# Three elementwise instructions of a weight quantiser, moved from VectorE to GpSimd beside attention

## The reference, cut to what matters

```python
def _weight_quant(w):                       # w_gate, w_up: 4096 x 1024, w_down: 1024 x 4096
    scale = 1.0 / clip(mean(abs(w)), 1e-05)
    wq = clip(round(w * scale), -1.0, 1.0) / scale
    return w + stop_gradient(wq - w)
def _act_quant(x):
    scale = 127.0 / clip(max(abs(x), axis=-1), 1e-05)
    return clip(round(x * scale), -128.0, 127.0) / scale     # the value of it
def _bitlinear(x, w): return einsum('bsi,oi->bso', _act_quant(x), _weight_quant(w))

xn = layernorm(x)
attn = softmax(q k^T / 16) v @ Wo.T         # 8 heads of 256; k, v from a latent of 64
ffn  = _bitlinear(silu(_bitlinear(xn, w_gate)) * _bitlinear(xn, w_up), w_down)
out  = x + attn + ffn
```

## Time and profile before

| | us |
|---|---|
| median of 2 runs | 5789.53 (5685.05 and 5894.02) |
| profiled execution | 5426.39 |
| its span, slowest core | 5424.8 |
| spans of the 8 cores | 5410.8 to 5424.8 |
| PE busy in the span | 4204.7 |
| DVE busy | 2171.8 |
| ACT busy | 2088.7 |
| POOL busy | 602.9 |

### The profile page before, as it was taken

How to read it: one execution, slowest core, us unless ns; L and a number is a source line. 1 busy time by engine, 2 the same in 40 slices (tenths; PEclk the granted TensorE clock), 3 DMA queues, 4 the chain that set the end, 5 groups by cost and what they waited for, 6 DMA issues and landing times.

```text
span 5424.8 us, 91608 instructions; the slowest of 8 cores (5410.8 to 5424.8 us)
## 1 busy us (share of the span) xinstructions
PE 4204.7 (78%) x24244; PEld 2326.7 (43%) x24244; DVE 2171.8 (40%) x2977; ACT 2088.7 (39%) x3427; POOL 602.9 (11%) x517
## 2 busy tenths in 40 slices
PE   1123399797997989979899795688888888099999
PEld 1121156364563645636456363343444433044444
DVE  5545511313113131131321311599999999111111
ACT  4324466263562635626356263233333333000000
POOL 1000000000000000000000000233333333000000
PEclk8556599898998989979899898898998989599999
DMA  4664311011110111101111212111111111355454
GB/s 126 156 159 125 130 35 44 26 44 36 34 44 26 44 36 34 44 26 44 36 34 44 80 52 63 47 36 40 32 38 40 30 40 28 76 160 134 123 130 109
DMA packets 535678, 350.52 MB, mean 65 GB/s; under 512 B 441920, under 2 KB 486976, under 8 KB 535168
## 3 DMA queue, kind: packets, MB, share of 16 engines
q1 hardware_dynamic: 464736, 155.77, 12.1%
q0 software_dynamic: 31824, 92.95, 6.7%
q10 hardware_dynamic: 38608, 95.96, 5.3%
HBM read 244.61 MB, written 109.05 MB: 65 GB/s over the span
## 4 chain that ended last, share of the span: by engine, by line
PE 60%; DVE 20%; DMA 7%; issue 7%; ACT 4%; SPq 1%; DVEq 1%; ACTq 0%; POOLq 0%; POOL 0%
PE psF L763 17%; PE psF L752 16%; PE psF L1061 8%; PE psF L395 4%; PE psF L939 4%; PE psF L945 3%; DMA arC<-x 3%; PE psF L1047 3%; DVE rsc L480 3%; DVE rsc L477 3%; DVE arB L483 2%; DVE t L471 2%; ACT arB L778 2%; DVE arB L445 2%; DVE smf L963 2%
## 5 line engine op out<-in xcount | busy, mean ns | idle before, releaser
L757 ACT ACTIVATE arB<-psF 128x512 bf16<-128x512 f32 x2048 | 1216.0, 597 | 1283.5 <-PE psF L752 1062.5
L763 PE MATMUL psF<-arB 128*128 128x257 bf16 x8192 | 1280.7, 278 | 97.1 <-ACT arB L778 95.0
L752 PE MATMUL psF<-arB 128*128 128x512 bf16 x4096 | 1237.8, 390 | 18.3 <-DVE arB L445 18.3
L763 PEld LDWEIGHTS psF<-arB 128*128 128x128 bf16 x8192 | 782.3, 99 | 537.6 <-issue 178.6
L945 PE MATMUL psF<-arB 128*128 128x512 bf16 x2048 | 493.4, 385 | 75.1 <-DMA arB<-wuT_d 75.1
L939 PE MATMUL psF<-arA,arB 128*128 128x512 bf16 x2048 | 536.1, 409 | 6.4 <-DMA arB<-xnqT_d 6.4
L959 POOL TENSOR_TENSOR arC<-arC 128x512 f32<-128x512 f32 x256 | 425.7, 1663 | 831.5 <-ACT arC L956 831.5
L1061 PE MATMUL psF<-arB,arA 128*128 128x512 bf16 x2048 | 451.0, 381 | 71.1 <-DMA arB<-wdT_d 70.9
L772 DVE RECIPROCAL smf<-psF 128x1 f32<-128x1 f32 x256 | 43.1, 168 | 1123.0 <-PE psF L763 1103.3
L752 PEld LDWEIGHTS psF<-arB 128*128 128x128 bf16 x4096 | 408.3, 100 | 108.9 <-issue 28.4
L951 ACT ACTIVATE arC<-psF,smf 128x512 f32<-128x512 f32 x256 | 175.9, 687 | 714.6 <-PE psF L945 614.5
(11 more groups left out here) (125 smaller groups left out, 3533.4 us busy)
## 6 DMA issues: line engine op xcount, KB each, us to landing
hqT_d<-p1b SPq DMA_DIRECT2D x32, 1024.0 KB, 6.2
arA<-hqT_d SPq DMA_DIRECT2D x32, 1024.0 KB, 7.0
arC<-Wg ACTq DMA_DIRECT2D x32, 512.0 KB, 5.9
arC<-x SPq DMA_DIRECT2D x32, 512.0 KB, 7.3
arC<-Wu ACTq DMA_DIRECT2D x32, 512.0 KB, 6.9
arC<-Wd ACTq DMA_DIRECT2D x32, 512.0 KB, 4.8
arC<-Wg POOLq DMA_DIRECT2D x32, 512.0 KB, 5.3
aoT_d<-arB SPq DMA_DIRECT2D x64, 256.0 KB, 2.8
```

The costliest lines, as they stand in the source:

```text
L752: p.add("tensor", lambda e, bi=bi, c=c, g=g, d2=d2: e.matmul(bank(g), kT[:, d2 * T + c * 128: d2 * T + (c + 1) * 128], qT[:, d2 * T + bi * ...
L757: p.add("scalar", lambda e, g=g, c=c: e.activation(pT[c % 3][:, :], bank(g), AF.Exp, bias=0.0, scale=ISCL), reads=[b_bank[g]], writes=[b_p ...
L763: p.add("tensor", lambda e, c=c, sub=sub: e.matmul(pv_ps(sub, 0, 257), pT[c % 3][:, sub * 128:(sub + 1) * 128], vA[:, c * 257:(c + 1) * 25 ...
```

## The change

In `emit_passB1` the engine of the three operations is changed from "vector" (DVE) to "gpsimd" (POOL), for all 96 tiles. Operands, types, shapes, buffers and the place in the list stay as they are. The load L713 and the store L828 were issued from POOL already.

```diff
@@ -713,13 +713,13 @@
             p.add("gpsimd", lambda e, r=r, cb=cb, bb=bb, wsrc=wsrc: e.dma_start(
                 out=xst[bb][:, :], in_=wsrc[r * 128:(r + 1) * 128, cb * 1024:(cb + 1) * 1024]),
                 writes=[b_xst[bb]], dma=True)
-            p.add("vector", lambda e, bb=bb, bslot=bslot: e.tensor_scalar(
+            p.add("gpsimd", lambda e, bb=bb, bslot=bslot: e.tensor_scalar(
                 nn32[:, :], xst[bb][:, :], scw3[bslot], -0.5, op0=ALU.mult, op1=ALU.is_lt),
                 reads=[b_xst[bb], b_scw3[bslot]], writes=[b_nn])
-            p.add("vector", lambda e, bb=bb, bslot=bslot: e.tensor_scalar(
+            p.add("gpsimd", lambda e, bb=bb, bslot=bslot: e.tensor_scalar(
                 ee32[:, :], xst[bb][:, :], scw3[bslot], 0.5, op0=ALU.mult, op1=ALU.is_gt),
                 reads=[b_xst[bb], b_scw3[bslot]], writes=[b_ee])
-            p.add("vector", lambda e, bb=bb: e.tensor_tensor(
+            p.add("gpsimd", lambda e, bb=bb: e.tensor_tensor(
                 p1b[:, bb * 1024:(bb + 1) * 1024], nn32[:, :], ee32[:, :],
                 op=ALU.subtract),
                 reads=[b_nn, b_ee], writes=[ro])
```

## The result

| | us |
|---|---|
| profiled execution, before and after | 5426.4 and 5485.1 |
| mean span of the 8 cores, before and after | 5418.1 and 5467.5 |
| ratio of the times, after to before | 1.009 (95% interval 1.0069 to 1.0111) |
| median of all 11 runs after, of 10 runs before | 5488.9 and 5824.2 |

The changed kernel is 0.9% slower, about 49 us. The two medians of all runs cannot be compared: in part of the executions of either kernel one die runs at a lower granted clock (0.77 to 0.81 instead of 0.86 to 0.88 in the longest ones) and the time is up to 9% longer, so the ratio is taken from undisturbed runs, which are 5431.9 and 5432.7 us before and 5474 to 5489 us after (mean 5482).

What follows compares the result with a forecast made beforehand. PE was taken to set attention's pace. Seven head ends cost 1.4 us, the eighth gained 1.2, inside heads nothing: 0 us on 5426, carried to the timed runs' median as 5790 us; range 5415 to 5950 us.

Steps and rivals of the forecast that it cites:

- Where the change could act: Attention's head ends, where transposes L816 wait on copy L797 behind the moved DVE instructions: 16.9 us in 8 waits.
- C: Time of one tile's three instructions on POOL: 6.2 us (comparisons 1.7 each, subtraction 2.5), with ends 5.3 and 14.1.
- comparisons over 3.8 us: Sign that would make the prediction wrong: POOL comparisons in attention taking over 3.8 us each; 1.7 us was forecast.
- the sign of the wait: L816 waiting on POOL: 0 to 3 us forecast at head ends; waits inside heads would make the prediction wrong.
- The formula: Change at a head's end: 2 x (5.8 + C) - 23.8 us, at best -1.17; forecast +0.2 us.
- load and wake: Per tile, before POOL's arithmetic: 5.3 us from the load's issue to its landing, plus 0.5 us to wake.
- the third: Attention: DVE disturbs POOL, C becomes 9.5 us, +54 us, 5844 us; no chance of its own given.
- rival 2: PE before L816, after a pair: POOL becomes the bound; from C = 10.4 about 110 us; chance 0.17 beyond that.
- 8 to 10.4: Range of C in us on POOL, whether disturbed by DVE or not; chance 0.13.
- The gain of 1.17 us: At each head's end, copy L797 starts earlier without DVE's six instructions ahead: 1.17 us each, 9.4 us for 8.
- The level: Whole kernel: 5426 us from the profiled execution, carried to the two timed runs' median, 5789.5, giving 5790 us.
- the likeliest case: C of 5.5 to 8 us on POOL: a change of -9 to +25 us, chance 0.45.

## Why the prediction was wrong, point by point

- **Where the change could act** was right: the head ends are the only place of gain, and of the loss. L797 moved to 0.10 us after L790, the wait on it fell from 16.9 to 7.5 us (forecast 8), L713 went out one by one, blocks inside heads had no more than a rare wait (none to two a core, 1.7 us at most), and the stage behind attention did not differ (1329.1 and 1329.3 us).
- **The step that failed is C**, "what C is". I took 1.7 us for a comparison and bounded it from above, short of a disturbance, with the two-input row: "at most the same (2.51)". It takes 3.70, while the two-input subtraction takes 2.12 (I had 2.5). C is 9.67 (933.61 to 943.28), not 6.2. So the pair was not ready after 24.0 us, just in time for 23.8, but after 28.1 (28.6 on average), and L816 waited 6.1 to 8.8 us where 0 to 3 were forecast. The prediction's own sign "comparisons over 3.8 us" did not quite come; the sign of the wait did. A row of one operation bounded neither another operation nor even a simpler-looking one on POOL: a lone multiply costs 2.85.
- **The formula held.** With C = 9.67 it gives 2 x 15.47 - 23.8 = 7.1 us an end and 0.6 us for each of 24 pairs inside: 50 + 15 - 1.2 = +64 us. Measured were 5.1 us an end and almost nothing inside, since load and wake took 4.95 and 3.90 us at the first end (928.66 to 933.61, 943.22 to 947.12), 5.2 and 4.2 on average, and not 5.8. Both terms were too large. The wake was 0.5 us, from a DMA issue behind a DVE copy; from a landing to the comparison it is about 0.1 us. The landing was 5.3 us, the median of all loads before, of which two thirds went out in twos; before, a single load landed after 4.9 us, the two of a pair after 5.3 and 6.0. Now the first of a pair lands after 4.9 us and the second, issued 15.7 us behind the last store instead of 1.4, after 4.0 (medians of 8 cores). The one error hides part of the other: C was 3.5 us too small, load and wake 0.6 and 1.6 us too large.
- **The rivals.** The time came out at the number of the third (+54 us, C = 9.5), but not by its cause: L716 took 3697 to 3707 ns in all of attention on every core, so nothing disturbed it. That the number fits is luck. It is rival 2, POOL late, below its point of decision (10.4), and by C the case "8 to 10.4", to which I gave 0.13. By the Trainium skill (SBUF — State Buffer, "Who interferes with whom") DVE's copies from PSUM should not have disturbed POOL, and that spread agrees.
- **The Trainium skill** (GPSIMD Engine Reference, section 3.1) led to an estimate of 5.3 us for C, further off than mine. Its two-input figure fits the bf16 subtraction (2.22 us by that estimate against 2.12 measured), though it was low for the float32 product L959 (1109 against 1255 ns at least); its section 4.1, that one-input work is "roughly line-rate", fits the copy (1.04 us) and not the comparison (3.70).
- **The gain of 1.17 us** an end is real (0.96 and 1.03 in two experiments), but "-9 us" in the time is not: both ended at 1.000. The step left out the clock, which takes 0.6 of about 1.0 us back in the next 6 us; the 0.4 us left at each end, 3 us in all, are too little to measure. So the term at the seven ends was mis-sized too, though it is small beside C.
- **The level.** Carrying the sum from 5426 onto the median of two runs was a guess; the runs from which the ratios are taken agree with the profiled execution within 0.2%. The sum belonged where it was made. The stated range of 5415 to 5950 us holds the measured median only because it spans both levels, and is no support for the sum: on one level the likeliest case's range was -9 to +25 us, and +49 lies outside it.

## What to carry to other kernels

Price every operation on GpSimd by its own row; where there is none, leave a wide range, whatever another operation costs there (the one-input forms tried here took 1.04 to 3.71 us at one size). When work moves to an engine that also issues its loads, count the pair from the first issue to the last result: the second load waits for the first one's arithmetic, and two issues ahead of the arithmetic won back more than half of the loss. And before moving work off an engine, read who waits for it: here 210 us of DVE time were worth 9 us at most, and one wait elsewhere in the same list was worth about 60.

## What the runs showed of the hardware that I had not expected

- On POOL, `tensor_scalar` over 128x1024 costs 1.04 to 1.11 us as multiply-add, 2.85 as a multiply alone, 2.79 as a comparison alone, and 3.63 to 3.71 as multiply and compare. Adding a step made it two and a half times as fast.
- The granted clock stays at its lower level past the end of an idle stretch of PE. Of 1 us taken from an 8.9 us gap about 0.6 us came back as slower matmuls (the start grew from 71.24 to 71.82 and 71.85 us in the two kernels with the shorter gap, and the clock's cost in its first 6 us from 1.61 to 2.21 and 2.18), while a gap of 3.8 us cost less than before (0.55 us, start 70.30).
- Kernels whose blocks do the same work differed by up to 13 us in the sum of 56 blocks (1831 to 1844 us) from the granted clock alone: with the clock's part taken off, all nine profiles of such kernels lie within 1.4 us (1786.4 to 1787.8).
